# Three batch norm parameter sets, the split of one output weight, and the order in which a one-core perceiver block meets them

## The chip, the cores and the metric

The kernel runs on one core of a Trainium2 chip. The time is the device time of one launch in microseconds (us); the profile is of one such execution and is read on that core. Four compute engines matter: TensorE (PE in the profile, its weight loads PEld), VectorE (DVE), ScalarE (ACT) and GpSimd (POOL). SyncE (SP) issues most of the DMAs. Each engine runs its own program in order, and semaphores tie them together.

## The reference

A perceiver block in fp32: cross attention to a context, then an attention with batch norms and sigmoids (called self attention below), then a mixture of experts. Cut to what matters here:

```python
x = x + xattn(layernorm(x), ctx, mask, Wq, Wkv, Wo, qn_w, kn_w)    # x: 32 x 32 x 512
x = x + attn(layernorm(x), Wq, gq, bq, mq, vq, Wk, gk, bk, mk, vk, Wv, gv, bv, mv, vv, Wo, bo)
x = x + ffn(layernorm(x), gate_w, w1, w2, w3)

def attn(x, ...):
    def proj(x, W, g, b, m, v):
        h = x @ W
        h = (h - m) * (g * rsqrt(v + 1e-5)) + b
        return sigmoid(4.0 * (h - 1.0))
    Q, K, V = proj(x, ...q), proj(x, ...k), proj(x, ...v)
    delta = (1 - Q.mean(-1)) - (1 - K.mean(-1)).T          # per sequence
    f = 0.9 * exp(-abs(delta) / 0.5)
    A = where(delta < 0, f, -f) + 0.9
    return A @ V @ Wo + bo
```

The vectors g, b, m and v of each projection have 512 elements. With a = g * rsqrt(v + eps), the kernel scales the columns of W by a and subtracts c = m * a - b afterwards.

## The kernel before, in words

**Split products.** Every fp32 product is made of three: an operand is split into a high part (a rounded copy, made by ScalarE) and a low part (the difference, made by VectorE or GpSimd), and `split_products` (line 27) multiplies high by high, high by low and low by high. A product of 128 rows with a 512 x 512 weight is 12 matmuls of 128x512.

**The three stages.** Rows are handled in `TILES` = 8 tiles of 128 (four sequences each). Stage one runs over the 32 sequences, one `batch` each; a batch mixes the scores and the softmax of the sequence before with the key projection of the next. After the last of them `batch(TILES, 0, main=False, nxt=False)` ends the softmax of sequence 31 and begins `project(t)`: the cross attention's output product for tile t, for t = 0 to 7. Stage two (self attention) has `z_product(n)` for n = 0 to 23: n = 0 to 7 the query projections of the eight tiles, 8 to 15 the keys, 16 to 23 the values. Results rotate through three PSUM banks, so `z_product(n)` waits until VectorE has taken z(n-3) out of its bank (`z_c`). Stage three routes rows to experts and runs 23 slots of 128 rows.

**Around `project(0)`.** It needs the output weight `xo` split (four chunks c of 128 rows: high by ScalarE in `high_part`, low by VectorE at L1186 for c = 0, 1 and by GpSimd in `low_part`, L478, for c = 2, 3) and its left operand for tile 0 split: high by ScalarE in `out_high(0)` (L807), low by GpSimd in `out_low(0)` (L541). In ScalarE's program `out_high(0)` stands after the two copies `z_high` (L782) of the last batch. The split tile 0 lies on a buffer that the last but one context product still reads.

**Around the batch norms.** `bn_vec` holds the four vectors of one projection, each spread over 128 partitions (256 KB a vector). There is one such buffer. For w = 0, 1, 2 (queries, keys, values): SyncE loads the four vectors; ScalarE's `bn_root(w)` (L800, L802) makes rsqrt by Ln and Exp; VectorE's `bn_scale(w)` (L1205) makes a and `bn_shift(w)` (L1209, L1211) makes c, after which `bn_c` counts one more; GpSimd scales the weight by a (`bn_weight`, L549). SyncE waits for `bn_c` to reach w before it loads set w (line 411), since the buffer is one. `bn_root(2)` stands behind the whole layer norm loop in ScalarE's program, ahead of its 24 sigmoids. Sigmoids need another activation table than Ln and Exp, and the load of it stands ahead of the first sigmoid (L856). VectorE takes z(n) out of PSUM at L1293 into one of two buffers `sq`, and waits for the sigmoid of n-2 to be done with it. The four high parts of the key weight `ak` stand behind the sigmoids of n = 0 to 3.

**Memory.** Buffers are placed by hand with byte offsets (`at`). What sets the order of all work is the order in which each engine's program is written, with its waits.

## Time and profile before

| what | us |
|---|---|
| median of 3 runs | 795.37 (792.91 to 795.52) |
| the profiled execution | 794.86 |
| its span in the profile | 793.1 |
| TensorE busy in the span | 748.5 (94%) |
| VectorE, ScalarE, GpSimd busy | 551.7, 494.6, 240.6 |
| mean granted TensorE clock | 0.977 of full speed |

The span is counted from the first to the last instruction of the profiled execution; 1.8 us of its time lie around it. A row of the timeline gives its start in us from the start of the span, its length in us, the engine, the line, the operation, the output and the inputs, how many instructions it merges (x12), and, in square brackets, how long the engine stood idle just before and what ended that.

### The profile page before, as it was taken

The numbers are of one execution on the slowest core, as the hardware profiler recorded it, in microseconds if no ns is written. First come the engines' busy times: TensorE is split into PE (matmuls) and PEld (weight loads), VectorE is DVE, ScalarE is ACT, GpSimd is POOL, SyncE is SP. The second block draws the span as 40 slices with busy tenths as digits, with TensorE's granted clock in tenths as the row PEclk, the third lists the DMA queues.
The fourth block names the chain that finished last, engine by engine and source line by source line (L and its number), as shares of the span: only waits on it lengthen the run. The fifth ranks groups of instructions, "written<-read, shape, count | busy, mean of one in ns | idle before, by whom it ended". The sixth has DMA issues, their size and how long they took to land.

```text
span 793.1 us, 13557 instructions
## 1 busy us (share of the span) xinstructions
PE 748.5 (94%) x4501; PEld 652.5 (82%) x4501; DVE 551.7 (70%) x1045; ACT 494.6 (62%) x1089; POOL 240.6 (30%) x183
## 2 busy tenths in 40 slices
PE   4898999999999999999999997998999948999996
PEld 3687899999999898999999996986788846888875
DVE  6877886776867768867768675874567763655573
ACT  4666786785767768857857676537655422655660
POOL 2562212121211112121212123832780003555545
PEclk9999999999999999999999999999999957999999
DMA  9831211212121212112211404344016383466658
GB/s 300 83 120 40 68 54 40 80 56 63 40 79 40 79 40 75 44 40 79 63 56 46 127 1 110 93 142 148 1 52 202 118 305 92 83 111 108 114 80 317
DMA packets 59671, 75.18 MB, mean 95 GB/s; under 512 B 8784, under 2 KB 33360, under 8 KB 59632
## 3 DMA queue, kind: packets, MB, share of 16 engines
q1 hardware_dynamic: 52032, 58.16, 24.8%
q0 software_dynamic: 4720, 11.27, 7.9%
q10 hardware_dynamic: 2880, 5.24, 1.8%
q8 instruction: 22, 0.36, 0.2%
q14 instruction: 17, 0.14, 0.1%
HBM read 54.75 MB, written 19.92 MB: 94 GB/s over the span
## 4 chain that ended last, share of the span: by engine, by line
PE 80%; DVE 9%; ACT 4%; DMA 3%; issue 2%; POOL 1%; SPq 0%; POOLq 0%; ACTq 0%; DVEq 0%
PE pK L32 37%; PE pV L32 13%; PE pP L32 11%; PE pS L32 6%; PE pT L1508 3%; PE pT L1689 3%; PE pP L1672 2%; PE pT L1803 1%; DMA fin<-total 1%; DMA bn_vec<-in_L_attn_vv_dram 1%; DVE bst L965 1%; PE pS L1757 1%; DMA total<-big,idx 1%; PE pT L1488 1%; PE pS L1824 1%
## 5 line engine op out<-in xcount | busy, mean ns | idle before, releaser
L32 PE MATMUL pK<-parts 128*128 128x512 f32 x840 | 211.9, 400 | 2.2 <-POOL parts L541 2.2
L510 POOL TENSOR_TENSOR parts<-big,parts 128x1024 fp32r<-128x1024 f32 x32 | 77.7, 2429 | 338.2 <-ACT parts L735 338.2
L32 PEld LDWEIGHTS pK<-parts 128*128 128x128 f32 x840 | 153.3, 190 | 31.1 <-POOL parts L541 2.4
L32 PE MATMUL pK<-w,lhs 128*128 x276 | 70.7, 406 | 1.7 <-DVE lhs L1425 1.5
L32 PEld LDWEIGHTS pK<-w,lhs 128*128 128x128 f32 x276 | 51.3, 193 | 13.1 <-issue 3.0
L1007 DVE TENSOR_TENSOR kn<-pK,head_rs 128x512 f32<-128x512 f32 x62 | 42.7, 688 | 20.1 <-ACT head_rs L637 19.5
L763 ACT ACTIVATE pT<-pP 128x512 fp32r<-128x512 f32 x32 | 19.2, 599 | 56.8 <-PE pP L1672 56.8
L1441 DVE TENSOR_TENSOR w_p<-big,w_p 128x1024 fp32r<-128x1024 f32 x22 | 27.0, 1226 | 39.5 <-ACT w_p L922 39.5
L32 PE MATMUL pS<-kT,qblk 128*128 128x258 f32 x384 | 51.3, 283 | 2.1 <-DVE qoT L1041 2.1
L32 PE MATMUL pP<-pT,parts 128*128 128x256 f32 x384 | 51.6, 283 | 0.0
L32 PE MATMUL pK<-w_a,xT 128*128 128x512 f32 x192 | 47.8, 404 | 3.0 <-DVE sq L1293 3.0
L32 PEld LDWEIGHTS pS<-kT,qblk 128*128 128x128 f32 x384 | 48.1, 189 | 2.3 <-DVE qoT L1041 2.3
L575 POOL DMA_INDIRECT big<-x_rows,idx_x x23 | 25.6, 1114 | 78.3 <-DVE idx_x L1415 62.5
L32 PEld LDWEIGHTS pP<-pT,parts 128*128 128x128 f32 x384 | 46.3, 188 | 3.6 <-issue 0.8
L32 PE MATMUL pV<-pT,parts 128*128 128x256 f32 x384 | 49.1, 277 | 0.0
L631 ACT ACTIVATE sq<-pK 128x512 f32<-128x512 f32 x62 | 37.1, 598 | 15.4 <-PE pK L32 15.4
L996 DVE TENSOR_TENSOR parts<-pT,parts 128x512 fp32r<-128x512 f32 x62 | 39.7, 682 | 9.8 <-ACT parts L627 9.8
L32 PEld LDWEIGHTS pK<-w_a,xT 128*128 128x128 f32 x192 | 36.8, 194 | 11.5 <-issue 3.9
L32 PEld LDWEIGHTS pV<-pT,parts 128*128 128x128 f32 x384 | 46.2, 188 | 0.0
L1181 DVE TENSOR_TENSOR kT<-pT,kT 128x512 fp32r<-128x512 f32 x62 | 40.0, 687 | 8.7 <-ACT kT L774 8.5
L1001 DVE TENSOR_REDUCE head_ss<-sq 128x8 f32<-128x512 f32 x62 | 42.2, 681 | 4.2 <-ACT sq L631 3.1
L581 POOL DMA_INDIRECT total<-big,idx x20 | 31.7, 1586 | 42.1 <-ACT big L936 42.1
(318 smaller groups left out, 1623.8 us busy)
## 6 DMA issues: line engine op xcount, KB each, us to landing
big<-in_ctx_dram SPq DMA_DIRECT2D x32, 512.0 KB, 3.8
total<-zero SPq DMA_DIRECT2D x32, 256.0 KB, 4.0
w_raw<-in_L_ffn_w_dram SPq DMA_DIRECT2D x16, 512.0 KB, 6.7
big<-in_L_ffn_w_dram SPq DMA_DIRECT2D x8, 512.0 KB, 8.0
fin<-total SPq DMA_DIRECT2D x8, 512.0 KB, 7.2
big<-in_L_xattn_Wkv_dram SPq DMA_DIRECT2D x2, 1024.0 KB, 11.2
x_rows<-big ACTq DMA_DIRECT2D x8, 256.0 KB, 2.1
total<-big ACTq DMA_DIRECT2D x8, 256.0 KB, 2.3
```

The source lines that it names most:

```text
L32: last = pe.matmul(out, lhs(a, c), rhs(b, c), start=start and c == first and n == 0, stop=stop and c == chunks - 1 and n == 2)
L510: nc.gpsimd.tensor_tensor(ctxN[:, u, LO], ctx_raw[:, u], ctxN[:, u, HI].bitcast(F32), ALU.subtract).then_inc(cn_lo, 1)
L575: nc.gpsimd.indirect_dma_start(xg[:, j % 2, :], None, x_rows[:, :], bass.IndirectOffsetOnAxis(idx_x[:, j:j + 1], 0), bounds_check=T - 1).t ...
L581: nc.gpsimd.indirect_dma_start(total[:, :], bass.IndirectOffsetOnAxis(idx[:, j:j + 1], 0), y_sb[:, j % 2, :], None, bounds_check=5 * T - 1 ...
L631: act.activation(sq[:, t], pKV[t][:, :], ACT.Square).then_inc(k_sq, 1)
L996: tt(ctxT[:, u, LO, :, t * P:(t + 1) * P], pTT[t][:, :, :], ctxT[:, u, HI, :, t * P:(t + 1) * P].bitcast(F32), ALU.subtract).then_inc(ctx_ ...
L1001: nc.vector.tensor_reduce(head_ss[:, t], heads(sq[:, t]), AX.X, ALU.add).then_inc(k_ss, 1)
L1007: tt(heads(kn[:, t]), heads(pKV[t][:, :]), per_head(head_rs[:, t]), ALU.mult).then_inc(k_n, 1)
L1181: tt(kT[:, LO, :, t * P:(t + 1) * P], pTT[t][:, :, :], kT[:, HI, :, t * P:(t + 1) * P].bitcast(F32), ALU.subtract).then_inc(k_lo, 1)
L1441: tt(w2_buf(j)[:, LO], w2_all[:, bass.ds(e, 1)].rearrange("p e c n -> p (e c) n"), w2_buf(j)[:, HI].bitcast(F32), ALU.subtract).then_inc(w ...
L1508: last = pe.transpose(pTT[t][:, c, :], ctx_raw[:, u, t, c * P:(c + 1) * P], ident[:, :])
L1689: last = pe.transpose(pTT[t][:, c, :], kn[:, t, c * P:(c + 1) * P], ident[:, :])
```

## The change

There are two edits, each in several engines' programs.

**The output weight and the first tile.** The four chunks of `xo` are split in the order 3, 0, 1, 2. GpSimd makes the low part of chunk 3 alone, VectorE those of 0, 1 and 2. `out_high(0)` moves ahead of the last batch's two `z_high` copies, behind a wait for the context products that still read its buffer.

**The batch norms.** The key vectors get a place of their own, `bn_vec_k`, on memory that the cross attention's last batch used; SyncE loads them when that batch's transposes and sums are over, ahead of the wait on `bn_c`. The value vectors then take the old place as soon as the query vectors are used up. The load of experts 0 and 1 comes after both. `bn_root(2)` moves into the layer norm loop, behind t = 6, and the sigmoid table is asked for behind t = 8. Since `bn_vec_k` overlaps the key weight's high part, each of its four high parts now waits for `bn_c` to reach 2. `high_count` and the wait in `load_weight` are adapted to the new order of chunks.

```diff
--- before.py
+++ after.py
@@ -180,6 +180,7 @@
         w_a = at("w_a", [P, 2, 2, C, D], 96 * KB, F32R)
         xn3 = wide[:, 0:2 * C * D].rearrange("p (t d) -> p t d", t=TILES)
         bn_vec = at("bn_vec", [P, 4, D], 128 * KB)
+        bn_vec_k = at("bn_vec_k", [P, 4, D], 109 * KB + 8256)
         lhs2 = at("lhs2", [P, 2, 2, C, P], 128 * KB, F32R)
         v_self = qoT[:, :, :].rearrange("p c n -> p (c n)").rearrange("p (t d) -> p t d", t=TILES)
 
@@ -250,7 +251,8 @@
         w_lo = [sem(f"w_lo_{j}") for j in JOBS]
         raw_in = lambda name: (w_in[JOBS.index(name) % 2], 16 * (JOBS.index(name) // 2 + 1))
         w_hi, w_centred, w_scaled = sem("w_hi"), sem("w_centred"), sem("w_scaled")
-        high_count = lambda name, c: JOBS.index(name) * 4 + c + 1
+        XO_ORDER = (3, 0, 1, 2)
+        high_count = lambda name, c: JOBS.index(name) * 4 + (XO_ORDER.index(c) if name == "xo" else c) + 1
         w_sum = sem("w_sum")
         ln_bst, ln_mv, ln_lg, ln_rsd, ln_x, ln_t, ln_hi, ln_lo = (sem(n) for n in (
             "ln_bst", "ln_mv", "ln_lg", "ln_rsd", "ln_x", "ln_t", "ln_hi", "ln_lo"))
@@ -308,6 +310,7 @@
         }
         JOB = {n: i for i, n in enumerate(JOBS)}
         bn_src = ((gq, bq, mq, vq), (gk, bk, mk, vk), (gv, bv, mv, vv))
+        bn_of = (bn_vec, bn_vec_k, bn_vec)
         bn_ac = ((bn_a0[:, :], bn_c0[:, :]),
                  (bn_k[:, 0, :], bn_k[:, 1, :]),
                  (qkw[:, 0, :], qkw[:, 1, :]))
@@ -356,7 +359,7 @@
                 j = JOB[name]
                 if freed_by is not None:
                     sp.wait_ge(w_lo[JOB[freed_by]], C)
-                    sp.wait_ge(w_hi, high_count(freed_by, C - 1))
+                    sp.wait_ge(w_hi, 4 * (JOBS.index(freed_by) + 1))
                 sp.dma_start(raw(name), jobs[name][0]).then_inc(raw_in(name)[0], 16)
 
             zeros_of_row = zero[:, :].unsqueeze(1).broadcast_to([P, C, P])
@@ -407,14 +410,17 @@
                 for lo, w in ((0, w1), (F, w3)):
                     sp.dma_start(w13_raw[e][:, :, lo:lo + F], chunked(w[e])).then_inc(w13_in[e % 4], 16)
 
-            for w in range(1, 3):
-                sp.wait_ge(bn_c, w)
-                for i in range(4):
-                    sp.dma_start(bn_vec[:, i, :], spread(bn_src[w][i])).then_inc(bn_in[w], 16)
-                if w == 1:
-                    sp.wait_ge(o_mm, 2 * TILES)
-                    load_expert(0)
-                    load_expert(1)
+            sp.wait_ge(k_t, B * MT)
+            sp.wait_ge(p_t, B)
+            sp.wait_ge(p_rs, B)
+            for i in range(4):
+                sp.dma_start(bn_vec_k[:, i, :], spread(bn_src[1][i])).then_inc(bn_in[1], 16)
+            sp.wait_ge(bn_c, 1)
+            for i in range(4):
+                sp.dma_start(bn_vec[:, i, :], spread(bn_src[2][i])).then_inc(bn_in[2], 16)
+            sp.wait_ge(o_mm, 2 * TILES)
+            load_expert(0)
+            load_expert(1)
             sp.wait_ge(xo_mm, TILES)
             load_expert(2)
             load_weight("av", "aq")
@@ -549,7 +555,7 @@
                 nc.gpsimd.tensor_tensor(raw(name)[:, c], raw(name)[:, c], bn_ac[w][0],
                                         ALU.mult).then_inc(w_scaled, 1)
 
-            low_part("xo", range(C // 2, C))
+            low_part("xo", XO_ORDER[:1])
             for t in range(TILES):
                 if t == C:
                     for c in range(C):
@@ -775,7 +781,9 @@
                 if nxt:
                     k_square(b + 1, 0)
                 if main and not nxt:
-                    high_part("xo")
+                    high_part("xo", XO_ORDER)
+                    act.wait_ge(pc_mm, (b - 1) * 2 + 2)
+                    out_high(0)
 
                 def z_high(g):
                     act.wait_ge(pc_mm, (b - 1) * 2 + 2 - g)
@@ -797,9 +805,9 @@
 
             def bn_root(w):
                 act.wait_ge(bn_in[w], 64)
-                act.activation(bn_vec[:, 3, :], bn_vec[:, 3, :], ACT.Ln, bias=BN_B).then_inc(bn_lg, 1)
+                act.activation(bn_of[w][:, 3, :], bn_of[w][:, 3, :], ACT.Ln, bias=BN_B).then_inc(bn_lg, 1)
                 act.wait_ge(bn_lg, w + 1)
-                act.activation(bn_vec[:, 3, :], bn_vec[:, 3, :], ACT.Exp, scale=-0.5).then_inc(bn_rs, 1)
+                act.activation(bn_of[w][:, 3, :], bn_of[w][:, 3, :], ACT.Exp, scale=-0.5).then_inc(bn_rs, 1)
 
             def out_high(t):
                 if t >= 2:
@@ -813,7 +821,6 @@
                     batch(k, r)
             for r in range(BT):
                 batch(TILES - 1, r, nxt=r < BT - 1)
-            out_high(0)
             out_high(1)
             batch(TILES, 0, main=False, nxt=False)
 
@@ -834,7 +841,10 @@
                 if t == 3:
                     bn_root(1)
                     act.wait_ge(zeroed, 16 * B)
-            bn_root(2)
+                if t == 6:
+                    bn_root(2)
+                if t == TILES:
+                    act.preload_act_table_set("sigmoid_and_others")
 
             def w13_high(e, part=slice(0, C)):
                 act.wait_ge(w13_in[e % 4], 32 * (e // 4 + 1))
@@ -858,6 +868,7 @@
                 else:
                     act.activation(v_self[:, t], sq[:, n % 2], ACT.Sigmoid, bias=SIG_B, scale=SLOPE).then_inc(z_sig, 1)
                 if n < C:
+                    act.wait_ge(bn_c, 2)
                     high_part("ak", (n,))
                 if TILES + 3 <= n < TILES + 3 + C:
                     high_part("av", (n - TILES - 3,))
@@ -1181,7 +1192,7 @@
                         tt(kT[:, LO, :, t * P:(t + 1) * P], pTT[t][:, :, :],
                            kT[:, HI, :, t * P:(t + 1) * P].bitcast(F32), ALU.subtract).then_inc(k_lo, 1)
                 if main and not nxt:
-                    for c in range(C // 2):
+                    for c in XO_ORDER[1:]:
                         dve.wait_ge(w_hi, high_count("xo", c))
                         tt(xo_p[:, LO, c], raw("xo")[:, c], xo_p[:, HI, c].bitcast(F32),
                            ALU.subtract).then_inc(w_lo[JOB["xo"]], 1)
@@ -1202,13 +1213,13 @@
 
             def bn_scale(w):
                 dve.wait_ge(bn_rs, w + 1)
-                tt(bn_ac[w][0], bn_vec[:, 0, :], bn_vec[:, 3, :], ALU.mult).then_inc(bn_a, 1)
+                tt(bn_ac[w][0], bn_of[w][:, 0, :], bn_of[w][:, 3, :], ALU.mult).then_inc(bn_a, 1)
 
             def bn_shift(w):
                 dve.wait_ge(bn_a, w + 1)
-                tt(bn_vec[:, 2, :], bn_vec[:, 2, :], bn_ac[w][0], ALU.mult).then_inc(bn_ma, 1)
+                tt(bn_of[w][:, 2, :], bn_of[w][:, 2, :], bn_ac[w][0], ALU.mult).then_inc(bn_ma, 1)
                 dve.wait_ge(bn_ma, w + 1)
-                tt(bn_ac[w][1], bn_vec[:, 1, :], bn_vec[:, 2, :], ALU.subtract).then_inc(bn_c, 1)
+                tt(bn_ac[w][1], bn_of[w][:, 1, :], bn_of[w][:, 2, :], ALU.subtract).then_inc(bn_c, 1)
 
             def out_add(t):
                 dve.wait_ge(xo_mm, t + 1)
```

On ScalarE at the end of the last full batch: the four high parts of `xo` (parts<-big), the copies of the context products (w_p), the high parts of the output tiles (parts<-qoT), then the softmax. Before:

```order
L622 ACTIVATE parts<-big 128x512 [waits w_in1] x4
L782 ACTIVATE w_p<-pP 128x16x32 [waits pc_mm]
L782 ACTIVATE w_p<-pV 128x16x32 [waits pc_mm]
L807 ACTIVATE parts<-qoT 128x512 x2
L745 ACTIVATE prob,p_sum<-s_m,neg_max 128x257 [waits p_t,sc_max]
```

The same place now:

```order
L628 ACTIVATE parts<-big 128x512 [waits w_in1] x4
L815 ACTIVATE parts<-qoT 128x512 [waits pc_mm]
L790 ACTIVATE w_p<-pP 128x16x32 [waits pc_mm]
L790 ACTIVATE w_p<-pV 128x16x32 [waits pc_mm]
L815 ACTIVATE parts<-qoT 128x512
L751 ACTIVATE prob,p_sum<-s_m,neg_max 128x257 [waits p_t,sc_max]
```

The high part of tile 0 has moved ahead of the two copies, with a wait for the context products. On VectorE at the same place, the low parts of `xo` and the two low parts of the context products, before:

```order
L1181 TENSOR_TENSOR kT<-pT,kT 128x4x128 [waits k_hi] x2
L1186 TENSOR_TENSOR parts<-big,parts 128x512 [waits w_hi] x2
L1194 TENSOR_TENSOR w_p<-pP,w_p 128x16x32 [waits pc_hi]
L1194 TENSOR_TENSOR w_p<-pV,w_p 128x16x32 [waits pc_hi]
L1132 SCALAR_TENSOR_TENSOR s_m<-mask_f,pS 128x2x257 [waits sc_mm]
```

The same place now:

```order
L1192 TENSOR_TENSOR kT<-pT,kT 128x4x128 [waits k_hi] x2
L1197 TENSOR_TENSOR parts<-big,parts 128x512 [waits w_hi] x3
L1205 TENSOR_TENSOR w_p<-pP,w_p 128x16x32 [waits pc_hi]
L1205 TENSOR_TENSOR w_p<-pV,w_p 128x16x32 [waits pc_hi]
L1143 SCALAR_TENSOR_TENSOR s_m<-mask_f,pS 128x2x257 [waits sc_mm]
```

One more low part stands ahead of the softmax. On ScalarE at the end of the layer norm loop (ln_log and ln_rs are the root for a tile, xT<-pT its high part) and at the first sigmoids (big,rows<-sq), before:

```order
L611 ACTIVATE xT<-pT 128x4x128 [waits ln_t]
L605 ACTIVATE ln_log<-mean_var,bias 128x1 [waits ln_mv]
L607 ACTIVATE ln_rs<-ln_log 128x1 [waits ln_lg]
L611 ACTIVATE xT<-pT 128x4x128 [waits ln_t] x3
L800 ACTIVATE bn_vec<-bn_vec,bias 128x512 [waits bn_in2]
L802 ACTIVATE bn_vec<-bn_vec 128x512 [waits bn_lg]
L856 ACT_TABLE_LOAD [waits ln_t]
L856 ACTIVATE big,rows<-sq,bias 128x512 [waits z_c]
L622 ACTIVATE w_a<-big 128x512 [waits w_scaled]
```

The same place now:

```order
L617 ACTIVATE xT<-pT 128x4x128 [waits ln_t]
L808 ACTIVATE bn_vec<-bn_vec,bias 128x512 [waits bn_in2]
L810 ACTIVATE bn_vec<-bn_vec 128x512 [waits bn_lg]
L611 ACTIVATE ln_log<-mean_var,bias 128x1 [waits ln_mv]
L613 ACTIVATE ln_rs<-ln_log 128x1 [waits ln_lg]
L617 ACTIVATE xT<-pT 128x4x128 [waits ln_t] x2
L847 ACT_TABLE_LOAD
L617 ACTIVATE xT<-pT 128x4x128 [waits ln_t]
L866 ACTIVATE big,rows<-sq,bias 128x512 [waits ln_t,z_c]
L628 ACTIVATE w_a<-big 128x512 [waits w_scaled,bn_c]
```

The two roots and the table load have moved from between the last layer norm tile and the first sigmoid to places further up; there is still one table load.

## Rows read from the trace of the kernel before

**Rows 1.** The page: busy time of TensorE; its granted clock in 40 slices.

```profile
PE 748.5 (94%) x4501; PEld 652.5 (82%) x4501; DVE 551.7 (70%) x1045; ACT 494.6 (62%) x1089; POOL 240.6 (30%) x183
PEclk9999999999999999999999999999999957999999
```

**Rows 2.** Windows: from:to, length, busy PE, PEld, DVE, ACT, POOL, clock, DMA.

```profile
476.00:480.00 4.00, 1.94 (x13) 1.25 (x13) 2.57 (x7) 2.99 (x9) 0.58 (x1) 1.00 0.00 0
487.50:490.50 3.00, 3.00 (x9) 2.32 (x8) 1.08 (x4) 0.91 (x2) 0.58 (x1) 0.50 0.91 264
542.00:545.00 3.00, 3.00 (x9) 2.33 (x8) 0.92 (x2) 3.00 (x8) 3.00 (x4) 0.50 0.00 0
550.00:573.00 23.00, 23.00 (x103) 19.05 (x102) 13.77 (x13) 14.61 (x32) 12.44 (x8) 1.00 0.02 8
```

**Rows 3.** Timeline 481 to 495, all engines: the wait ahead of project(0), and after.

```profile
481.04 2.20 ACT L622 ACTIVATE parts<-big 128x512 fp32r<-128x512 f32 x4
481.90 1.28 DVE L1186 TENSOR_TENSOR parts<-big,parts 128x512 fp32r<-128x512 f32 x2
482.79 2.81 POOL L478 TENSOR_TENSOR parts<-big,parts 128x512 fp32r<-128x512 f32 x2 [6.21 <-ACT parts L622]
483.10 1.60 PE L32 MATMUL pS<-kT,qblk 128*128 128x258 f32 x12
483.60 0.61 ACT L782 ACTIVATE w_p<-pV 128x512 fp32r<-128x512 f32 x1
484.08 1.16 ACT L807 ACTIVATE parts<-qoT 128x512 fp32r<-128x512 f32 x2
484.95 0.68 DVE L1132 SCALAR_TENSOR_TENSOR s_m<-mask_f,pS 128x514 f32<-128x514 uint8 x1
485.56 2.52 POOL L541 TENSOR_TENSOR parts<-qoT,parts 128x512 fp32r<-128x512 f32 x2
486.88 7.37 PE L32 MATMUL pK<-parts 128*128 128x512 f32 x24 [2.18 <-POOL parts L541]
488.53 0.91 ACT L752 ACTIVATE prob<-prob,p_scale 128x256 f32<-128x256 f32 x2 [1.04 <-DVE p_scale L1147]
491.53 0.63 ACT L807 ACTIVATE parts<-qoT 128x512 fp32r<-128x512 f32 x1 [2.09 <-PE pK L32]
492.24 1.30 POOL L541 TENSOR_TENSOR parts<-qoT,parts 128x512 fp32r<-128x512 f32 x1 [4.16 <-ACT parts L807]
494.66 2.98 PE L32 MATMUL pK<-parts 128*128 128x512 f32 x12
```

**Rows 4.** Timeline, VectorE: two inputs in SBUF, GpSimd idle, then busy.

```profile
498.55 0.68 DVE L1205 TENSOR_TENSOR bn_a<-bn_vec 128x512 f32<-128x512 f32 x1
504.65 1.79 DVE L1209 TENSOR_TENSOR bn_vec<-bn_vec,bn_a 128x512 f32<-128x512 f32 x1
```

**Rows 5.** Timeline 509 to 546, all engines; the first row is a DMA's issue.

```profile
509.51 0.43 SPq L413 DMA_DIRECT2D bn_vec<-in_L_attn_vk_dram  x1
516.46 0.71 ACT L800 ACTIVATE bn_vec<-bn_vec,bias 128x512 f32<-128x512 f32 x1
522.69 0.60 ACT L611 ACTIVATE xT<-pT 128x512 fp32r<-128x512 f32 x1 [1.13 <-PE pT L1488]
531.21 0.68 DVE L1293 TENSOR_TENSOR sq<-pV,bn_c 128x512 f32<-128x512 f32 x1
535.27 2.88 PE L32 MATMUL pK<-w_a,xT 128*128 128x512 f32 x12
536.70 0.72 ACT L800 ACTIVATE bn_vec<-bn_vec,bias 128x512 f32<-128x512 f32 x1 [6.13 <-DMA bn_vec<-in_L_attn_vv_dram]
540.32 0.69 DVE L1293 TENSOR_TENSOR sq<-pK,bn_c 128x512 f32<-128x512 f32 x1 [7.82 <-ACT big L856]
541.15 4.58 PE L32 MATMUL pK<-w_a,xT 128*128 128x512 f32 x12 [3.01 <-DVE sq L1293]
545.58 2.90 PE L32 MATMUL pV<-w_a,xT 128*128 128x512 f32 x12
```

## The prediction, as it was made before the changed kernel had run

> **What bounds the kernel now.** I read the page first: TensorE is busy 94% of the span, and its granted clock dips in one place of the 40 slices [rows 1]. So time goes only where TensorE waits, or where it runs at a lower clock. The wait view of TensorE and finer windows of the clock, read next around the two edits, show two such places, which the 40 slices hide. One is ahead of project(0): TensorE ends the last scores at 484.7 (483.10 + 1.60) and idles 2.18 us until GpSimd has the low part of tile 0, and then project(0) and project(1) take 7.37 us together [rows 3]. The other is ahead of the sixth query projection, z(5): TensorE ends z(4) at 538.15, idles 3.01 us for VectorE, and z(5) takes 4.58 us where z(4) took 2.88 [rows 5]. In both cases the granted clock after the wait is 0.50, the lower of the two levels (1.2 of 2.4 GHz), for the whole of a 3 us window [rows 2]. After two shorter waits it is not: between 476 and 480 TensorE is busy 1.94 of 4.00 us, in pieces, and the clock stays at 1.00 [rows 2]. Further on, from 550 to 573, TensorE is busy 23.00 of 23.00 us, so what comes earlier at z(5) stays earlier there [rows 2]; the rest of the program hangs on TensorE's results by semaphores and moves with it.
>
> **The change at z(5).** Before, the chain is: the value vectors are asked for late, their root is at 536.70 after 6.13 us in which ScalarE waited for the DMA, then the second half of the root, then the table load, the first sigmoid, and VectorE at 540.32, which had waited 7.82 us for a free `sq` buffer, and TensorE at 541.15 [rows 5]. VectorE had the first z out of PSUM at 531.89 (531.21 + 0.68) [rows 5].
> - Removed ahead of the first sigmoid: the wait, the two root passes and the table load. ScalarE can begin the sigmoid at about 531.9. Its third result is wanted at 538.15; with sigmoid and a key weight's high part at about 1.5 us a turn (0.9 + 0.6, from the sigmoids and splits that follow) there are some 4 us to spare.
> - Added: the wait for `bn_c` on the key weight's high parts. It is met: the same VectorE passes stood ahead of VectorE's own loop before, and 531.21 lies behind them. The low parts on GpSimd end at about 539, and the key projections want them at z(8), not before 546.
> - Moved: the roots stand behind ScalarE's pass at 522.69 + 0.60, so 1.35 us of work falls into a gap. The next root of a layer norm comes about 0.5 us later; VectorE is at its own batch norm passes then, so it isn't late. The DMA: the value vectors take the place in SyncE's queue that the key vectors had, whose last one was issued at 509.51 and was there when ScalarE came to it at 516.46 [rows 5]. So it is there at 523 too. The key vectors' four issues (0.43 us each) now stand ahead of a wait on SyncE that ends at 508 anyway. Experts 0 and 1 come as before, and the value weight some 7 us earlier.
> - The gain: the wait 3.01, the slow clock 4.58 - 2.88 = 1.70, and 0.15 by which one product overlaps the next (545.73 against 545.58) [rows 5]. Sum 4.9 us.
>
> **The change at project(0).** Before, the chain is: ScalarE's four chunks from 481.04, 0.55 us each; GpSimd's two low parts 482.79 to 485.60; its low part of tile 0 from 485.56; TensorE at 486.88. ScalarE had the high part of tile 0 only at about 484.66, behind two other copies [rows 3].
> - Now GpSimd has its one chunk after the first 0.55 us, from 481.6 to 483.0, and is free. ScalarE's tile 0 follows its four chunks and the context product, which ends where the scores start: 483.3 to 483.9. GpSimd takes 1.3 us, so 485.2. VectorE's third low part, at 0.64, ends by 484.2 if nothing hinders it. Project(0) would start at 485.2.
> - But the other bound. VectorE's pass over two SBUF inputs took 0.68 with GpSimd idle and 1.79 with GpSimd at work [rows 4]. If the two engines take turns here as well, VectorE begins after GpSimd's chunk, at 483.0, has two chunks at 484.3, and the last one and GpSimd's tile 0 follow one another: 484.3 + 1.3 + 0.6 = 486.2 for the start.
> - What is late next: the softmax. The two copies come 0.7 us later on ScalarE, so VectorE's mask pass moves from 484.95 to 485.7, or with the engines taking turns to 487.4. The scaled probabilities end 4.5 us behind it (484.95 to 489.44) [rows 3]: 490.2 or 491.9. Only then does ScalarE make the high part of tile 2 (0.63), GpSimd its low part (1.30), and project(2) may start: 492.1 or 493.8, against 494.66 [rows 3]. Project(0) and (1) at the full clock take 5.6 us (2.88 twice less 0.15) instead of 7.37 and end at 490.8 or 491.8, so project(2) is what waits.
> - The gain is 2.5 or 0.9 us, most of it the clock that isn't lost. The idle pieces (0.5 to 1.5 us ahead of project(0)) are like those of 476 to 480, which kept the clock [rows 2]. I take the middle, 1.6; both ends stay in the range.
>
> The Trainium skill ("SBUF — State Buffer", "Who interferes with whom") says that a VectorE instruction with two SBUF inputs contends with a GpSimd instruction that reads SBUF, and that the second to issue is blocked until the first ends. By that rule the second bound would hold and the gain here would be 0.9; the 1.79 of rows 4 agrees with it.
>
> **The sum.** 4.9 + 1.6 = 6.5 us. The profiled execution is 794.86 (span 793.1 and 1.8 around it), which gives 788.4; the median of the runs, 795.37, is 0.5 above it and gives 788.9. A change under 0.5% (4.0 us) can hardly be told from none here.
>
> **The rivals.**
> 1. **The clock is still lost at project(0).** The wait may stay near 1.5 us, and other pieces lie close to it (476 to 480), so together they may tell. Then project(0) and (1) take 7.4 us from 486.2 and project(2) starts at about 494.5: gain 0.2. For it: the high bound of that wait; against it: the clock kept in 476 to 480 [rows 2]. Time 795.37 - 4.9 - 0.2 = 790.3.
> 2. **Another wait takes the place of the one at z(5).** ScalarE's sigmoids share the engine with the key weight's splits, and GpSimd and VectorE are slower side by side; if TensorE still stands for over a microsecond and the clock is lost, 2.5 of the 4.9 are left. Against it: the 4 us to spare. Time 795.37 - 2.5 - 1.6 = 791.3.
> 3. **The clock later on.** The dip in the slices 33 and 34 [rows 1] lies in the routing. When it begins and ends may shift by up to 1.5 us either way, since everything is earlier by an amount that has nothing to do with it: 787.4 or 790.4.
> 4. **Slower: the value vectors land late, now in the middle of the layer norm loop.** Before, their wait stood where only the sigmoids were behind it; now the roots of a layer norm tile and its high part are behind it too, and TensorE at once behind these. Each us that they land after about 526 (523.3 and some slack on VectorE) costs one on TensorE, and the clock 1.7 more. Slower than before they make it from a landing at about 531. The experts' loads follow right behind them, as they did behind the key vectors, and these were there by 516.46 [rows 5]. Price at a landing of 533: about 797.
>
> **How the numbers follow.** The forecast 0.47, rival 1 0.20, rival 2 0.15, rival 3 0.13 (both ways), rival 4 0.05. Faster by over 0.5% means under 791.4: the forecast, rivals 1 and 3 and a fifth of rival 2, 0.83. Within: the rest of rival 2, 0.12. Slower: rival 4, 0.05. The range begins at the best of all bounds, 795.37 - 2.5 - 4.9 - 1.5 = 786.5, less 1 us since the median itself lies at the upper end of 792.91 to 795.52: 785.5. It ends past rival 2, at 792.0.
>
> **What would show it.** Right: no ACT wait ahead of bn_vec; first sigmoid at about 530 (1.6 us earlier by the first edit); z(0) to z(7) without a gap and at 1.00; project(0) starting between 485.2 and 486.2 and taking 2.9 us; project(2) at 492 to 494 behind GpSimd. Wrong: a clock of 0.50 in either place, a TensorE wait ahead of z(3) to z(8), or a wait of ScalarE for the value vectors in the layer norm loop. The forecast falls if an engine other than TensorE turns out to set the pace between 494 and 531, since then the first gain is given back there.

## The result and the profile after

| | median of runs (lowest to highest) | profiled execution | its span | its mean granted clock |
|---|---|---|---|---|
| before | 793.78 us (792.55 to 795.52), 5 runs | 794.86 us | 793.1 us | 0.977 |
| changed | 789.1 us (788.16 to 791.38), 5 runs | 791.38 us | 789.6 us | 0.977 |

The ratio is 0.9942, with a 95% interval of 0.9918 to 0.9966: faster by 4.7 us, and by over 0.5% of the time by the estimate, though the interval reaches to 0.34%. The forecast was 788.9. The two profiled executions are not the typical ones: that of before lies 1.1 above its median, that of the changed kernel is the slowest of its five. They differ by 3.5 us.

The page, engines and clock in 40 slices (answers to [rows 1]):

```profile
PE 748.8 (95%) x4501; PEld 653.6 (83%) x4501; DVE 552.7 (70%) x1046; ACT 494.8 (63%) x1089; POOL 238.8 (30%) x182
...
PEclk9999999999999999999999999999999957999999
```

TensorE's busy time is the same to 0.3 us. What went is idle time of TensorE; the time lost to the slow clock has moved rather than gone. The two longest waits of TensorE from 470 to 560, as engine, line, releaser, sum, number and longest:

```profile
PE pP L1683 <- ACT prob L758: 1.5, 1, 1.5
PE pK L32 <- POOL parts L547: 0.7, 1, 0.7
```

The wait of 3.01 for `sq` is no longer there, and that for GpSimd ahead of project(0) went from 2.18 to 0.66 [rows 3, 5]. (Those of 1.48 and 0.57 stand in both kernels.) The edit on the output weight in the timeline of all engines (columns as in [rows 3]; "..." stands for rows left out; line numbers of the changed kernel are 6 to 11 higher):

```profile
480.37 2.90 PE L32 MATMUL pP<-pT,parts 128*128 128x256 f32 x12
...
481.92 1.30 POOL L484 TENSOR_TENSOR parts<-big,parts 128x512 fp32r<-128x512 f32 x1 [5.27 <-ACT parts L628]
482.39 2.58 DVE L1197 TENSOR_TENSOR parts<-big,parts 128x512 fp32r<-128x512 f32 x3 [0.33 <-ACT parts L628]
...
484.72 1.60 PE L32 MATMUL pS<-kT,qblk 128*128 128x258 f32 x12
484.92 0.63 ACT L815 ACTIVATE parts<-qoT 128x512 fp32r<-128x512 f32 x1 [1.53 <-PE pV L32]
...
485.63 1.30 POOL L547 TENSOR_TENSOR parts<-qoT,parts 128x512 fp32r<-128x512 f32 x1 [2.42 <-ACT parts L815]
...
486.98 5.72 PE L32 MATMUL pK<-parts 128*128 128x512 f32 x24 [0.66 <-POOL parts L547]
...
487.27 0.68 DVE L1143 SCALAR_TENSOR_TENSOR s_m<-mask_f,pS 128x514 f32<-128x514 uint8 x1
...
491.94 1.30 POOL L547 TENSOR_TENSOR parts<-qoT,parts 128x512 fp32r<-128x512 f32 x1 [3.53 <-ACT parts L815]
...
493.30 1.89 PE L32 MATMUL pK<-parts 128*128 128x512 f32 x7
```

The order is the one described: one low part on GpSimd, three on VectorE, tile 0's high part ahead of the other two copies. Project(0) and (1) take 5.72 instead of 7.37. But the first context product, at 480.37, takes 2.90. In the profile of before it took 1.60:

```profile
480.30 1.60 PE L32 MATMUL pP<-pT,parts 128*128 128x256 f32 x12
```

There the scores started at 483.10 [rows 3], here at 484.72. The slow clock is now on that product. In the windows (columns as in [rows 2]; the number behind POOL's is the granted clock):

```profile
480.50:483.50 3.00, 3.00 (x16) 3.00 (x15) 2.40 (x3) 2.89 (x6) 1.30 (x1) 0.50 0.02 5
...
487.50:490.50 3.00, 3.00 (x15) 2.45 (x14) 1.70 (x6) 1.16 (x5) 0.92 (x1) 1.00 0.36 118
530.00:538.00 8.00, 8.00 (x37) 6.62 (x36) 3.26 (x5) 5.55 (x13) 5.14 (x4) 1.00 0.00 0
```

The first is at 1.2 GHz (0.50), the other two at 2.4. The stretch at z(5), as an answer to [rows 5], first the last issue of the value vectors, then ScalarE, then TensorE from z(3) on (x24 is two products in a row, z(4) and z(5)):

```profile
507.98 0.43 SPq L420 DMA_DIRECT2D bn_vec<-in_L_attn_vv_dram  x1
...
521.89 0.71 ACT L808 ACTIVATE bn_vec<-bn_vec,bias 128x512 f32<-128x512 f32 x1
...
525.95 1.28 ACT L847 ACT_TABLE_LOAD   x1
...
530.62 0.73 ACT L866 ACTIVATE big<-sq,bias 128x512 f32<-128x512 f32 x1 [1.36 <-DVE sq L1304]
...
531.22 2.88 PE L32 MATMUL pV<-w_a,xT 128*128 128x512 f32 x12
533.94 5.60 PE L32 MATMUL pK<-w_a,xT 128*128 128x512 f32 x24
539.38 2.88 PE L32 MATMUL pV<-w_a,xT 128*128 128x512 f32 x12
```

The value vectors' root starts at 521.89 with no wait, the first sigmoid at 530.62 waits only for the first z, and TensorE goes through z(5) without a gap and at the full clock.

### The profile page after: what moved, and what is told of

It is laid out like the page before. It is cut to its first block, busy times and chain, and to the rows that moved or that the text cites. A ratio compares the mean times of both kernels' runs of the same rounds, so it can differ in the third digit from the quotient of the medians.

```text
span 789.6 us, 13562 instructions
## 1 busy us (share of the span) xinstructions
PE 748.8 (95%) x4501; PEld 653.6 (83%) x4501; DVE 552.7 (70%) x1046; ACT 494.8 (63%) x1089; POOL 238.8 (30%) x182
## 4 chain that ended last, share of the span: by engine, by line
PE 83%; DVE 7%; DMA 3%; ACT 3%; issue 2%; POOL 1%; SPq 0%; POOLq 0%; ACTq 0%; DVEq 0%
PE pK L32 38%; PE pV L32 14%; PE pP L32 11%; PE pS L32 6%; PE pT L1700 3%; PE pT L1519 3%; PE pP L1683 2%; DMA big<-x_rows,idx_x 1%; PE pT L1814 1%; DMA fin<-total 1%; PE pT L1499 1%; PE pS L1768 1%; DVE bst L976 1%; DMA total<-big,idx 1%; DVE head_mean L996 1%
## 5 line engine op out<-in xcount | busy, mean ns | idle before, releaser
L32 PE MATMUL pK<-w_a,xT 128*128 128x512 f32 x192 | 45.9, 393 | 0.0
L1178 DVE TENSOR_TENSOR pT<-pP,pT 128x512 fp32r<-128x512 f32 x32 | 22.1, 692 | 29.6 <-ACT pT L769 29.4
```

What stands on the lines that cost most here:

```text
L32: last = pe.matmul(out, lhs(a, c), rhs(b, c), start=start and c == first and n == 0, stop=stop and c == chunks - 1 and n == 2)
```

## Where the difference lies, stretch by stretch

Read from TensorE's timeline of each kernel, as the time from one landmark to the next. M is the start of the last full key product of the last batch (473.78 before); P the start of project(2); R the last layer norm tile's transposes, behind a wait of 1.64; S the second of the 23 `w,lhs` products, one of which opens each expert slot (R to S is called the routing below); Y the first product that gathers the experts' results (`y_p`). What the table leaves out (P to z(0) 28.50 to 28.58; z(0) to z(4) 12.06 to 12.12) is the same in all kernels in which nothing was edited there.

| kernel | M to P | z(4) to z(6) | z(6) to R | R to S | S to Y |
|---|---|---|---|---|---|
| before | 20.88 | 10.31 | 91.26 | 29.39 | 107.70 |
| changed | 19.46 | 5.44 | 91.27 | 30.87 | 108.63 |

The changed kernel leads by 1.4 us at project(2) and by 6.2 at z(6), and still has the 6.2 at R. It loses 1.5 in the routing and 0.9 in the expert slots, whose code is untouched, and 0.3 behind them: 3.5 are left. So two questions were put to further runs: what each edit is worth by itself, and whether these last losses, and the slow clock on the context product, come from the change or from the execution.

## The experiments

Ratios are to the kernel before, run in the same job on the same chip (medians 793.29, 794.21, 793.34 and 795.21 us in the four jobs: e1 to e4, e5 to e8, e9 to e11, e12). The ratio with its interval is an estimate of its own and not the quotient of the two medians; the two can differ by over a microsecond, and where they do, both are given. "The batch norm edit" is the one that e12's expectation calls the first part, "the output weight edit" the second.

### Each part alone

**e1** is the changed kernel with the output weights as before: only the batch norm part is left ("..." marks lines left out, here and below).

```
-        XO_ORDER = (3, 0, 1, 2)
-        high_count = lambda name, c: JOBS.index(name) * 4 + (XO_ORDER.index(c) if name == "xo" else c) + 1
+        high_count = lambda name, c: JOBS.index(name) * 4 + c + 1
...
-            low_part("xo", XO_ORDER[:1])
+            low_part("xo", range(C // 2, C))
...
-                    high_part("xo", XO_ORDER)
-                    act.wait_ge(pc_mm, (b - 1) * 2 + 2)
-                    out_high(0)
+                    high_part("xo")
...
+            out_high(0)
...
-                    for c in XO_ORDER[1:]:
+                    for c in range(C // 2):
```

> The batch norm part of the change alone. Theory A (the two parts add): the wait ahead of z(5) and its slow clock are gone, 4.9 us in the trace between project(0) and z(6), and the median is 4 to 5 us under the kernel before. Theory B (the gain needs the earlier start from the other part): under 3 us. In both the wait ahead of project(0) stays at about 2.2 us.

Measured: 788.45 us (6 runs), ratio 0.9921, interval 0.9900 to 0.9942. M to P 20.86, z(4) to z(6) 5.45. By the trace all of the gain at z(5) is there and none of that at project(0).

**e2** is the other half: the kernel before with the hunks that e1 takes back, so the norm vectors are loaded late as before.

```
-            low_part("xo", range(C // 2, C))
+            low_part("xo", XO_ORDER[:1])
...
-                    high_part("xo")
+                    high_part("xo", XO_ORDER)
+                    act.wait_ge(pc_mm, (b - 1) * 2 + 2)
+                    out_high(0)
...
-                    for c in range(C // 2):
+                    for c in XO_ORDER[1:]:
```

> The part on the output weight and the first tile alone. Theory A: project(2) starts 1.3 to 1.5 us earlier than before, with project(0) at the full clock, and the clock lost on the context products just ahead instead; z(5) still waits 3.0 us; the median 0 to 2 us under before. Theory B (it is the clock's position that costs, by chance): in this execution the clock may be kept on the context products as well, and then project(2) starts about 2.9 us earlier.

Measured: 792.83 us (12 runs), ratio 0.9976, interval 0.9958 to 0.9995. Its timeline of TensorE, and the window behind z(5)'s wait:

```profile
482.87 1.65 PE L32 MATMUL pP<-pT,parts 128*128 128x256 f32 x12
...
488.56 5.71 PE L32 MATMUL pK<-parts 128*128 128x512 f32 x24 [1.18 <-POOL parts L542]
...
540.42 2.98 PE L32 MATMUL pK<-w_a,xT 128*128 128x512 f32 x12 [2.24 <-DVE sq L1295]
```

```profile
541.00:544.00 3.00, 3.00 (x15) 2.48 (x14) 1.75 (x3) 3.00 (x8) 3.00 (x4) 1.00 0.03 10
```

Here the clock stays up on the context product (1.65) and at project(0) (5.71 for two), and M to P is 18.36, the full 2.5 us of the better bound. That is theory B. And, with the late loads untouched, z(5) waits 2.24 instead of 3.01 and takes 2.98 at clock 1.00 instead of 4.58: z(4) to z(6) is 7.95, not 10.31. So the cost that the batch norm edit removes is not 4.9 us in every execution. By the medians the two parts, 4.8 us (793.29 - 788.45) and 0.5, add up to about the whole, 4.7. By the ratios they are 6.3 and 1.9 (0.4 to 3.3 by the interval), which is more than the whole's 4.6. So the runs don't show that the parts simply add.

**e3** has only the early loads: the second root passes and the sigmoid table stay behind the layer norm loop, the output weights as before.

```
             act.wait_ge(zeroed, 16 * B)
-                if t == 6:
-                    bn_root(2)
-                if t == TILES:
-                    act.preload_act_table_set("sigmoid_and_others")
+            bn_root(2)
```

> The batch norm part without its moves on ScalarE: the key vectors have their own place, both loads are early, but the value root and the table load stand behind the layer norm loop as before. Theory A (the DMA was what z(5) waited for): the root runs right behind the last layer norm tile, at about 530.6, then the table load, so the first sigmoid is at about 533.4 and nothing reaches z(5): the same gain as with all of the part, 4 to 5 us. Theory B (the moves on ScalarE carry part of it): the third z comes out of PSUM over 1 us later than z(5) could start, a wait of 1 us or more stays, gain 2 to 4 us.

Measured: 789.37 us (6 runs), ratio 0.9935, interval 0.9915 to 0.9955. ScalarE's first sigmoid, and z(4) and z(5) on TensorE:

```profile
533.84 0.72 ACT L861 ACTIVATE big<-sq,bias 128x512 f32<-128x512 f32 x1
```

```profile
535.92 5.60 PE L32 MATMUL pK<-w_a,xT 128*128 128x512 f32 x24
```

The sigmoids start 1.2 us later than in the changed kernel by the distance to z(4) (2.1 ahead of it instead of 3.3), and TensorE notices nothing: 5.60 for two products, no wait. The early load alone gives the gain at z(5); moving the roots and the table only adds slack.

### Is it the clock

**e4** is the kernel before with 12 matmuls of no use ahead of z(5), into a PSUM buffer that is free there (`keep_warm` issues them). They fill the wait.

```
+                    if n == 5:
+                        pe.wait_ge(ln_lo, 2 * TILES - 1)
+                        keep_warm(pT0[:, :, :].rearrange("p c n -> p (c n)"), xT[:, HI, 0, 0:P], w_a[:, 0, HI, 0, :], 12)
```

> The kernel before, with 12 matmuls of 128x512 into a free PSUM bank, whose result nobody reads, in TensorE's wait ahead of z(5). Nothing waits less. Theory A (a wait of TensorE costs its length and then the lower clock): z(5) takes 2.9 instead of 4.6 us, the wait itself stays 3.0 (2.7 of it now filled), gain 1.7 us. Theory B (the lower clock has another cause, such as the DMA burst at 538 to 541): z(5) takes 4.6 us as before, no gain.

Measured: 793.78 us (12 runs), ratio 1.0001, interval 0.9982 to 1.0019.

```profile
538.60 2.89 PE L1496 MATMUL pT<-w_a,xT 128*128 128x512 f32 x12
541.32 2.91 PE L32 MATMUL pK<-w_a,xT 128*128 128x512 f32 x12
```

The fillers keep z(5) at 2.91, as theory A had it, but z(4) to z(6) is 8.19, no better than e2 had without any (7.95). Where the clock survives by itself the fillers give nothing, and the median shows no gain at all: 1.7 us in every execution would be a ratio of 0.9979, outside the interval.

**e5** is the changed kernel with such fillers in the three waits between 476 and 487 (5, 2 and 2 of them). **e7** is the changed kernel with 4, 9, 16 and 5 of them in the waits of the routing. Nobody reads what these matmuls write. One of e5's three places, then two of e7's four:

```
...
+                if main and not nxt:
+                    pe.wait_ge(pc_lo, b * 2 - 2)
+                    keep_warm(pP_flat, wkv[:, HI, 0, 0:P], wk(HI, 0), 5)
...
```

> The changed kernel with matmuls whose result nobody reads in TensorE's waits between 476 and 487 (5 ahead of the last batch's transposes of probabilities, 2 ahead of those of keys, 2 ahead of project(0)). Theory A (these waits together bring the lower clock, at the context products or at project(0), by the execution): the clock is 1.00 from 474 to 496 in the trace, and the mean time is 1 to 1.5 us under the changed kernel. Theory B (the lower clock there does not hang on TensorE's idle time): the clock is lost as before, and the time is the same.

```
+            def route_warm(count):
+                pe.wait_ge(x2_add, TILES)
+                pe.wait_ge(w13_lo, 1)
+                keep_warm(pK1[:, :], w13[:, 0, HI, 0, 0:P], w13[:, 0, HI, 0, :], count)
...
+            route_warm(9)
...
+            route_warm(16)
...
```

> The changed kernel with matmuls whose result nobody reads in TensorE's waits in the routing (4 ahead of the last layer norm tile's transposes, 9 ahead of the counts, 16 ahead of the slot products, 5 ahead of the first slot). Theory A (idle time brings the lower clock here too, for some 28 us): the clock stays at 1.00 or comes back sooner, the slot products of 3.6 us and the first slot's 4.6 to 5.5 us get shorter, 2 to 4 us under the changed kernel. Theory B (these waits are too long and the products between them too small, so that the clock falls at their begin and the added matmuls run at half speed): the same, or slower by up to 3 us.

Measured: e5 789.38 us (6 runs), ratio 0.9940, interval 0.9919 to 0.9961; e7 789.5 us (6 runs), 0.9946, interval 0.9929 to 0.9962. Neither differs from the changed kernel. In e5 the clock is kept where it was aimed at (context product 1.65, project(0) and (1) 5.76, M to P 18.42):

```profile
480.34 1.65 PE L32 MATMUL pP<-pT,parts 128*128 128x256 f32 x12
...
486.05 5.76 PE L32 MATMUL pK<-parts 128*128 128x512 f32 x24 [0.75 <-POOL parts L547]
```

Its R to S is 30.81, as long as in the changed kernel's profile (30.87), and its profiled execution is the shorter of the two by 1.1 us (790.29 against 791.38). So against that one profile the microsecond at project(0) is kept; over six runs the median doesn't show it. In e7, a filler group and the slot product behind the next wait:

```profile
633.71 3.83 PE L1507 MATMUL pK<-w 128*128 128x512 f32 x9
...
643.07 2.91 PE L1814 MATMUL pV<-tile_val,row_hot 128*128 128x24 f32 x16 [1.47 <-DVE row_hot L1416]
```

That slot product is faster (2.91, where the changed kernel and e6 have 3.59), but R to S is 27.95, which e1, e3, e6 and e8 (27.85 to 27.89) reach with no fillers. The mean granted clock of e7's six runs is 0.982 to 0.991, against 0.977 to 0.981 in the changed kernel's, and the time is no shorter: a higher mean clock that fillers bring is not time won.

### The two halves of the output weight edit

**e6** takes from the changed kernel only the place of tile 0's high part; **e8** only the split of the chunks.

```
                     high_part("xo", XO_ORDER)
-                    act.wait_ge(pc_mm, (b - 1) * 2 + 2)
-                    out_high(0)
...
+            out_high(0)
```

> The changed kernel with the high part of tile 0 back behind the two copies on ScalarE; the chunks keep the new order. Theory A (both halves of this edit are needed): the low part of tile 0 begins 1.1 us later, project(0) with it, and nearly all of the 0.4 us (at equal clock) to 1.4 us of this edit are gone. Theory B (the chunk order alone carries it): project(0) starts as in the changed kernel, and the time is the same.

```
-        XO_ORDER = (3, 0, 1, 2)
+        XO_ORDER = (0, 1, 2, 3)
...
-            low_part("xo", XO_ORDER[:1])
+            low_part("xo", (2, 3))
...
-                    for c in XO_ORDER[1:]:
+                    for c in (0, 1):
```

> The changed kernel with the chunks of the output weight split as before (order 0 to 3, two low parts on GpSimd), tile 0 early. Theory A (both halves are needed): GpSimd has its two chunks at 2.8 us behind the second high part, so the low part of tile 0 begins where it did before the change, and the gain of this edit is gone. Theory B (tile 0's early place alone carries it): project(0) starts as in the changed kernel.

Measured: e6 789.35 us (6 runs), ratio 0.9940, interval 0.9924 to 0.9956; e8 790.95 us (8 runs), 0.9959, interval 0.9939 to 0.9978. The rows of TensorE, e6 and then e8:

```profile
481.25 2.72 PE L32 MATMUL pP<-pT,parts 128*128 128x256 f32 x12
...
487.95 5.74 PE L32 MATMUL pK<-parts 128*128 128x512 f32 x24 [1.12 <-POOL parts L547]
```

```profile
488.60 7.36 PE L32 MATMUL pK<-parts 128*128 128x512 f32 x24 [2.19 <-POOL parts L547]
```

In e8 tile 0's high part is early and nothing is won (M to P 20.90, wait 2.19): GpSimd still has two chunks first. In e6 the split is new and tile 0's high part is late; M to P is 19.83 with the slow clock on the context product, which is what kernels with the old order have in that case (19.80 to 19.89, below). So in the trace each half alone gives nothing. The medians are too close to say so by themselves: e6 can't be told from the changed kernel. They also vary more than their intervals suggest: by the stretches of their traces e1 and e8 are alike (20.86 and 20.90, 5.45 and 5.44, 27.89 and 27.85), and yet their medians, from two jobs, are 2.5 us apart and their ratios 0.9921 and 0.9959.

### The same kernels again, and the slower rival

**e9** is the changed kernel and **e11** the kernel before, both with nothing edited.

> The changed kernel a second time, nothing edited. The low clock between 476 and 490 lay on the context products in its first profile and on project(0) in those of others. Theory A (where the clock is lost is decided by the execution, not by the code): the profile of this run may show project(2) at 19.5 or at 18.4 us behind the last full key product, the first slot's products may again take 5.4 or be back at 4.6, and the median is within 0.15% of 789.1, a ratio of 0.994. The segments that hang on waits alone don't move: z(4) to z(6) 5.44, z(0) behind project(2) 28.5. Theory B (the place of the low clock belongs to the code): the same figures as in the first profile, 19.46, 5.45 for the first slot's product, to within 0.1.

> The kernel before a second time, nothing edited, one profile. Theory A (the loss of the clock at z(5) and the length of the wait for the value vectors vary from one execution to another): z(4) to z(6) comes out between 7.9 and 10.4, not necessarily the 10.31 of the first profile; project(2) at 19.8 or 20.9 behind the last full key product. Theory B (they belong to the code): 10.31 and 20.88 again, to within 0.1.

Measured: e9 788.81 us (6 runs), ratio 0.9941, interval 0.9919 to 0.9962, M to P 19.26, z(4) to z(6) 5.45, R to S 29.39. e11, one run, 791.23 us, M to P 19.82, z(4) to z(6) 8.32, R to S 28.06. In e9, VectorE, GpSimd and TensorE:

```profile
480.58 1.60 PE L32 MATMUL pP<-pT,parts 128*128 128x256 f32 x12
...
482.50 3.69 DVE L1197 TENSOR_TENSOR parts<-big,parts 128x512 fp32r<-128x512 f32 x3 [0.24 <-ACT parts L628]
...
484.30 3.06 POOL L547 TENSOR_TENSOR parts<-qoT,parts 128x512 fp32r<-128x512 f32 x2 [0.96 <-ACT parts L815]
...
486.34 5.71 PE L32 MATMUL pK<-parts 128*128 128x512 f32 x24 [1.36 <-DVE parts L1197]
...
491.98 1.28 POOL L547 TENSOR_TENSOR parts<-qoT,parts 128x512 fp32r<-128x512 f32 x1 [4.62 <-ACT parts L815]
...
493.31 3.01 PE L32 MATMUL pK<-parts 128*128 128x512 f32 x12 [0.61 <-POOL parts L547]
```

And in e11, TensorE, and ScalarE's wait for the value vectors:

```profile
481.10 2.81 PE L32 MATMUL pP<-pT,parts 128*128 128x256 f32 x12
...
487.88 5.74 PE L32 MATMUL pK<-parts 128*128 128x512 f32 x24 [1.12 <-POOL parts L541]
...
540.13 3.00 PE L32 MATMUL pK<-w_a,xT 128*128 128x512 f32 x12 [2.59 <-DVE sq L1293]
```

```profile
535.67 0.72 ACT L800 ACTIVATE bn_vec<-bn_vec,bias 128x512 f32<-128x512 f32 x1 [5.69 <-DMA bn_vec<-in_L_attn_vv_dram]
```

The same code moves its slow clock: e11 has it on the context product where [rows 3] had it on project(0), and after a wait of 2.59 z(5) takes 3.00, where [rows 5] showed 4.58 after 3.01. e9 has it in neither place. So the slow context product of the changed kernel's profile doesn't belong to the change.

**e10** is the changed kernel with the value vectors asked for behind expert 2's load.

```
-            sp.wait_ge(bn_c, 1)
-            for i in range(4):
-                sp.dma_start(bn_vec[:, i, :], spread(bn_src[2][i])).then_inc(bn_in[2], 16)
             sp.wait_ge(o_mm, 2 * TILES)
...
             load_expert(2)
+            sp.wait_ge(bn_c, 1)
+            for i in range(4):
+                sp.dma_start(bn_vec[:, i, :], spread(bn_src[2][i])).then_inc(bn_in[2], 16)
             load_weight("av", "aq")
```

> The changed kernel with one edit: the value vectors are asked for behind expert 2's load instead of ahead of expert 0's, so about 521.9 instead of 506.7. Their root stays inside the layer norm loop. Nothing is left out. This tests the slower rival. If it holds (theory A): they land 7 to 8 us after the issue, about 529; ScalarE waits some 6 us ahead of the first root pass, with the root of layer norm tile 6 and its high part behind it; TensorE waits 3 to 5 us ahead of that tile's product, z(0) to z(6) start later by that, and the time is 3 to 5 us above that of the changed kernel, 792 to 794, so the whole gain at z(5) is gone. Theory B (ScalarE's and VectorE's slack in the loop covers it, or the transfer lands in 4 us since nothing else is in flight): under 1 us above the changed kernel.

Measured: 797.91 us (12 runs), ratio 1.0048, interval 1.0032 to 1.0064: slower than before, and 9.1 us above e9 of the same job. ScalarE, and then TensorE:

```profile
533.15 0.72 ACT L808 ACTIVATE bn_vec<-bn_vec,bias 128x512 f32<-128x512 f32 x1 [9.31 <-DMA bn_vec<-in_L_attn_vv_dram]
```

```profile
536.30 1.09 PE L1499 MATMUL pT<-ident,big 128*128 128x128 f32 x4 [6.39 <-DVE xT L991]
537.04 4.33 PE L32 MATMUL pK<-w_a,xT 128*128 128x512 f32 x12
```

The mechanism came as expected, the size didn't (3 to 5 us were expected): the vectors were asked for from 523.76 on and the last landed at about 533.1, 4 us later than the 529 expected. What was left behind the slack went through to TensorE: 6.39 of wait, and 0.5 and 1.3 more by which the transposes (1.09 for 0.63) and the product (4.33 for 2.99) ran slower, at clock 0.52 in the window of 537 to 540. That is 8.2 us. In the changed kernel the last of these vectors is asked for at 507.98, lands 6.6 us later, at 514.6, and is wanted at 521.89. So the batch norm edit has 7 us to spare there, and it needs the load to be early.

### All profiles side by side

| kernel | M to P | slow clock there | z(4) to z(6) | R to S |
|---|---|---|---|---|
| old order: before, e1, e8 | 20.88, 20.86, 20.90 | on project(0) | 10.31, early loads, early loads | 29.39, 27.89, 27.85 |
| old order: e3, e4, e11 | 19.89, 19.80, 19.82 | on the context product | early loads, 8.19 with fillers, 8.32 | 27.88, 27.99, 28.06 |
| new order: changed, e7, e10 | 19.46, 19.52, 19.49 | on the context product | 5.44, 5.44, 5.44 | 30.87, 27.95, 29.47 |
| new order: e2, e9 | 18.36, 19.26 | none | 7.95 late loads, 5.45 | 29.38, 29.39 |
| new order with fillers: e5 | 18.42 | none | 5.44 | 30.81 |

(Kernels with early loads have 5.44 or 5.45. e8, with the old split and tile 0 early, is counted as old order; e6, with the new split and tile 0 late, is left out and has 19.83 and 27.88.) R to S falls near 27.9, 29.4 or 30.8, each with different kernels, and with before in two of the three. What differs is how long the clock stays down. Two windows of the changed kernel and the same two of e6, then each one's first slot product:

```profile
630.00:640.00 10.00, 4.83 (x29) 4.65 (x29) 4.89 (x22) 4.51 (x7) 0.00 (x0) 0.52 0.82 296
...
656.00:661.00 5.00, 5.00 (x12) 3.91 (x13) 0.69 (x1) 0.17 (x1) 1.02 (x1) 0.50 0.37 108
```

```profile
655.88 5.45 PE L32 MATMUL pK<-w,lhs 128*128 x12 [0.34 <-DVE lhs L1436]
```

```profile
630.00:640.00 10.00, 2.97 (x29) 2.75 (x29) 6.06 (x28) 5.24 (x8) 0.00 (x0) 0.69 0.79 271
...
656.00:661.00 5.00, 5.00 (x21) 4.01 (x21) 0.48 (x1) 1.35 (x2) 0.87 (x2) 0.83 0.26 85
```

```profile
654.74 4.41 PE L32 MATMUL pK<-w,lhs 128*128 x12 [0.38 <-DVE lhs L1435]
```

The clock falls earlier in the changed kernel's profile (0.52 against 0.69) and comes back later (0.50 against 0.83), and the first slot's product takes 5.45 instead of 4.41. The two kernels are only about 1 us apart in their timelines there, which is less than either difference.

In this table R to S with the old order is 28.1 at most but for one profile (29.39), and with the new one never under 29.38, fillers in the routing apart. If that belonged to the new order, it would give back in the routing what it wins at project(0). **e12** is e1 again, nothing edited, to see.

> The first part alone (output weights as before) a second time, nothing edited. Open is whether the second part's gain at project(0) is given back in the routing. From the last layer norm tile's transposes to the second product of the first expert slot, five of six profiles with the old weights' order show 27.9 to 28.1 us and one 29.4, and all five with the whole new order and no fillers in the routing show 29.4 to 30.9. Theory A (the new order brings the routing into a worse place of the clock): this profile shows about 27.9 again, and the median is not above that of the changed kernel, 789.0 or less, a ratio of 0.994 or less, so that the second part adds nothing to the first. Theory B (the place of the clock is chance): it may show 29.4 as well, and the median is 1 us above the changed kernel's, about 790, a ratio of 0.9955.

Measured: 789.53 us (7 runs), ratio 0.9938, interval 0.9916 to 0.9961. M to P is 19.28, R to S 29.53:

```profile
489.18 5.74 PE L32 MATMUL pK<-parts 128*128 128x512 f32 x24 [2.09 <-POOL parts L546]
```

The old order has the long routing here too, so it isn't bound to the new one. And it has a third case at project(0): a wait of 2.09 and two products at the full clock. That the routing's length is pure chance isn't shown either, with two long ones in seven profiles of the old order and five in five of the whole new one (e7 aside): if the seven long ones fell on the twelve profiles blindly, all five would be among them about 3 times in 100. This rival, that the new order lengthens the routing, stays open. The runs of e1 and e12 together have a median of 789.25 us (13 runs), those of the changed kernel and e9 788.88 (11 runs): what the output weight edit adds to the batch norm edit is 0.4 us by medians and 0.2 by means, less than their spread can tell from nothing, and by the ratios (0.9921 and 0.9938 against 0.9942 and 0.9941) it adds nothing. Added to the kernel before (e2) it was 0.5 us by the medians and 1.9 by the ratio, whose interval just leaves out zero. Its net worth stays open between nothing and about two microseconds.

## Why the prediction was right, and where its sum was off

**The number.** 789.1 against 788.9 looks closer than the reasoning was. The sum said 6.5 us below a median of 795.37 that came from three runs; the comparison had 4.7 below 793.78. An offset too high by 1.6 and a gain too large by 1.8 made up for each other, which is luck.

**z(5): mechanism right, size true of one execution.** Every sign that was named came: no wait of ScalarE ahead of `bn_vec`, first sigmoid at 530.62, z(0) to z(7) without a gap at 1.00, value vectors in time. In the profiled pair the term is exact: 10.31 - 5.44 = 4.87, forecast 4.9. The step that was off is the sum of this gain, the wait 3.01, the slow clock 1.70 and 0.15: it took the wait and the clock of one trace as the kernel's. In the other traces with late loads and no fillers the difference is 8.32 - 5.44 = 2.9 (e11) and 7.95 - 5.44 = 2.5 (e2): the wait was 2.59 and 2.24, and the clock was not lost. What varied ahead of it is ScalarE's wait for the DMA of the value vectors, 6.13, 5.69 and 5.37 us, and behind that the time from the last vector's issue to its landing, 7.2, 6.8 and 6.4 us. The mean of the three gains is 3.4; with another 0.3 that e11 and e2 take from z(6) to R (91.56 and 91.58 against 91.26 and 91.27), for which no row shows a reason, it is 3.6.

**Project(0): right by its ends, wrong by its signs.** Its two bounds were a gain of 2.5 and 0.9, the middle 1.6 was taken. Measured 1.4 in the pair, but not as described: project(0) started at 486.98, later than the 486.2 at most, because the slow clock on the context product had put the scores at 484.72. That is rival 1 in another place: the clock was lost, ahead of project(0) and not on it. The step that was wrong is the argument that idle pieces like those of 476 to 480 keep the clock. It rested on one profile: behind these same pieces, 1.48 and 0.57 us long, the context product ran slow in seven of the thirteen profiles that have them. By the table the gain depends on where either kernel loses it: 20.87 to 18.36 is 2.5 where the new one keeps it (the better bound, e2), 20.87 to 19.26 is 1.6 in e9, and 19.83 to 19.49 is 0.3 where both lose it on the context product, which is below the lower bound of 0.9. The means, 20.20 of seven profiles with the old order and 19.22 of five with the new (e5, e6 aside), give 1.0; the medians of the runs, 0.4 and 0.5, are not at odds with that nor with less, and the gain may be given back in the routing.

**Engines taking turns.** The prediction's second bound was that VectorE's and GpSimd's passes over SBUF hinder each other. They do in every profile of the new order, with no slow clock on TensorE in e2 and e9. VectorE's three low parts take 2.57 to 2.59, where three in a row at 0.64 would be 1.9, and 3.69 in e9. Project(0) starts at nearly the same distance behind M in both, 12.23 in e2 and 12.29 in e9, which is 486.0 and 486.1 on the clock of [rows 3]: the 486.2 of the second bound and never the 485.2 of the first. What differs is the softmax, as that bound had it. In e9 VectorE is free 1.1 us later, so its mask pass starts 13.27 behind M instead of 12.16, and GpSimd's low part of tile 2 at 17.93 instead of 16.82; project(2) then waits 0.61 for it, where in e2 it waits for nothing. That is the 0.9 us between e2 and e9. The rule of the Trainium skill ("SBUF — State Buffer", "Who interferes with whom"), that the second of two such instructions is blocked until the first ends, agrees: in e9 VectorE's third low part started at 484.41, 0.11 after GpSimd's low part of tile 0, and took 1.78 instead of 0.68. Which of the two outcomes comes is a matter of 0.1 us: GpSimd's low part of tile 0 starts 10.25 behind M in e9 and 10.35 in e2. The middle that was forecast, 1.6, is what e9 gives and not what the second bound gave (0.9): its softmax took 0.4 less from the mask pass to the end of the scaled probabilities than the 4.5 in the sum, and the mask pass came 0.3 earlier. The forecast had neither, so this match is luck too.

**Another wait in its place (rival 2)** didn't come: no wait stands ahead of z(3) to z(8), and by e3 even 1.2 us later sigmoids would do.

**The clock later on (rival 3)** came, with its size: 1.5 us in the routing in the profiled pair. It was treated as one case among others; the runs show that the place and length of the slow clock vary from one execution to the next, in the routing, at z(5) and at project(0). That the last 0.9 and 0.3 us of the pair are of the same kind is only likely: S to Y is 107.2 to 108.8 over all kernels with the same code there, and no run isolates it.

**The slower rival** was priced as "about 797" at a landing of 533, and the rule behind it, one us for each that the vectors land after about 526 and 1.7 for the clock, is on the clock of [rows 5]. In e10 they landed at 533.1; ScalarE's high part ahead of them is at 523.24 there and at 522.69 in [rows 5], so on that clock the landing is 532.6, and the rule gives 6.6 + 1.7 = 8.3 us. TensorE's stretch shows 8.2: 6.39 of wait and 1.8 of slow clock. So this mechanism was priced right, though the case had only 0.05 of the chances. The median, 9.1 above e9's, has 0.9 more than that, for which nothing in the traces accounts.

**What adds up.** By the means of the traces the edits win 3.4 + 1.0 = 4.4 us where they stand (4.6 with the 0.3 behind z(6)); the medians say 4.7 (0.9942), and 4.5 in the repetition (793.34 - 788.81). That agrees, but not to better than a microsecond: the batch norm edit alone has 4.8 and 5.7 by its two medians and 6.3 and 4.9 by its two ratios (e1, e12), where three traces show 2.5 to 4.9. The forecast's 6.5 was the difference from an execution of before with both its worst cases in it (its span is 793.1, e11's 789.5). None of the variants is measurably faster than the changed kernel; e1's 788.45, the lowest median, was 789.53 the second time.
